# A decoder block on one core: VectorE's small operations set between the maxima of the cross loop, value copy and mask planes moved to ScalarE, value bias to GpSimd

## What is computed

```python
x = x + attn(layernorm(x), Wq, Wk, Wv, Wo)                 # 16 heads of 8, softmax(-arccosh(...))
qh, kh, vh = heads(q @ Wq.T + bq), heads(k @ Wk.T + bk), heads(k @ Wv.T + bv)
scores = einsum('bhqd,bhkd->bhqk', qh, kh) / sqrt(8)
scores = where(mask, scores, -1e9)
x = x + (softmax(scores) @ vh) @ Wo.T + bo                 # the cross block
logits = -dist2(x, keys) + x @ rw.T + rb
topv, topi = top_k(logits, 4); w = softmax(topv)
x = x + sum_j w_j * expert[topi_j](x)                      # gelu, 512 hidden
```

## Time and profile before

| | us |
|---|---|
| median of 3 runs | 865.53 (859.93 to 865.55) |
| the profiled execution | 859.28 |
| its span, first to last instruction | 857.5 |
| the cross loop, first to last of its exponentials (L861) | 376.9 to 646.8 |

### The profile page before, as it was taken

One profiled execution on the slowest core, in us unless ns is written; L12 is line 12 of the kernel. 1 busy time (PEld: TensorE's weight loads), 2 busy tenths in 40 slices (PEclk: granted clock), 3 DMA queues, 4 the chain that ended last, 5 costly groups with the idle time before them and its releaser, 6 DMA issues.

```text
span 857.5 us, 16692 instructions
## 1 busy us (share of the span) xinstructions
PE 713.5 (83%) x5462; PEld 474.6 (55%) x5504; DVE 657.5 (77%) x1662; ACT 578.5 (67%) x747; POOL 477.1 (56%) x578
## 2 busy tenths in 40 slices
PE   3435688797898786999999999999994399999996
PEld 1124455464565553554444444444342399999994
DVE  4669999999899899788788898888745255555554
ACT  2513899999999989245666766657562267777771
POOL 2134887967966797424232634645354366566663
PEclk9855555555555555659999999999997599999999
DMA  9980000000000300051050100000015222222228
GB/s 297 336 274 0 1 1 1 1 0 1 2 1 1 75 0 1 1 157 44 24 169 19 39 25 27 15 17 23 14 33 166 75 60 82 77 79 76 79 79 270
DMA packets 56868, 56.63 MB, mean 66 GB/s; under 512 B 9712, under 2 KB 49520, under 8 KB 56656
## 3 DMA queue, kind: packets, MB, share of 16 engines
q1 hardware_dynamic: 51728, 45.14, 17.9%
q0 software_dynamic: 5056, 10.43, 3.7%
HBM read 25.97 MB, written 29.57 MB: 65 GB/s over the span
## 4 chain that ended last, share of the span: by engine, by line
PE 54%; DVE 24%; issue 12%; POOL 3%; DMA 3%; ACT 2%; SPq 1%; DVEq 0%; POOLq 0%; ACTq 0%
PE ops L1232 7%; PE slot L1337 6%; DVE S_FB L1467 5%; PE slot L1208 5%; DVE S_YZ L1479 4%; PE bps L1350 4%; PE slot L1216 4%; PE ops L1350 4%; PE slot L1045 4%; PE ops L1068 3%; DVE X_junk L1530 3%; DVE S_YZ L1500 3%; PE tps L1194 3%; PE bps L1082 2%; PE bps L1124 1%
## 5 line engine op out<-in xcount | busy, mean ns | idle before, releaser
L606 POOL TENSOR_TENSOR S_YZ<-S_YZ 128x512 f32<-128x512 f32 x128 | 183.0, 1463 | 56.1 <-ACT S_YZ L810 55.9
L861 ACT ACTIVATE B_W<-slot 128x1024 f32<-128x1024 f32 x128 | 131.3, 1026 | 92.5 <-PE slot L1216 92.4
L1530 DVE CUSTOM_DVE_ANT_0 X_junk<-tps,X_MB 128x512 bf16<-128x512 f32 x240 | 156.2, 688 | 31.7 <-PE tps L1194 30.9
L759 POOL DMA_INDIRECT picks<-F_ROUT,F_GOAL x94 | 103.0, 1096 | 70.9 <-DVE F_ROUT L1877 50.2
L1045 PE MATMUL slot<-S_UQT,S_UKT 32*128 32x256 f32 x256 | 84.9, 477 | 52.9 <-DVE S_YZ L1479 52.1
L1045 PEld LDWEIGHTS slot<-S_UQT,S_UKT 32*128 32x128 f32 x256 | 56.7, 298 | 83.2 <-DVE S_YZ L1479 68.7
L1467 DVE TENSOR_SCALAR S_FB<-slot 128x512 f32<-128x512 f32 x128 | 84.6, 684 | 18.5 <-PE slot L1049 18.0
L725 POOL DMA_INDIRECT rows<-B_ROW,B_IDX x64 | 62.7, 980 | 50.3 <-DVE B_ROW L1601 24.2
L1479 DVE SCALAR_TENSOR_TENSOR S_YZ<-slot,S_FB 128x512 f32<-128x512 f32 x128 | 83.5, 683 | 1.9 <-DVE S_FB L1467 0.5
L1049 PE MATMUL slot<-S_GQT,S_GKT 32*128 32x256 f32 x256 | 84.8, 447 | 0.0
L1194 PE MATMUL tps<-X_KFT,X_QFT 24*128 24x512 f32 x240 | 78.7, 519 | 3.4 <-DVE X_MX L1530 1.1
(11 more groups left out here) (300 smaller groups left out, 1595.9 us busy)
## 6 DMA issues: line engine op xcount, KB each, us to landing
rows<-S_blank SPq DMA_DIRECT2D x17, 1040.0 KB, 12.4
F_RIN<-rows SPq DMA_DIRECT2D x47, 130.0 KB, 2.1
B_W<-w1T SPq DMA_DIRECT2D x16, 256.0 KB, 4.4
F_W<-w2T SPq DMA_DIRECT2D x16, 256.0 KB, 4.9
X_CT<-ctxT SPq DMA_DIRECT2D x8, 256.0 KB, 4.7
B_W<-picks SPq DMA_DIRECT2D x8, 256.0 KB, 8.9
B_W<-picks SPq DMA_DIRECT2D x4, 384.0 KB, 5.6
picks<-F_ROUT,F_GOAL POOLq DMA_INDIRECT x94
```

The costliest lines, as they stand in the source:

```text
L606: g.tensor_tensor(Y[:, n % YR], Y[:, n % YR], Zr[:, n % ZR], ALU.add).then_inc(f_rdy, 1)
L861: act.activation(W[:, at:at + 2, 2 * j:2 * j + 2, :].rearrange("p h t n -> p h (t n)"), E_BANKS[k % 2][:, :, :], ACT.Exp, scale=SCALE).the ...
L1530: dve.tensor_tensor_reduce(out=junk[:, i, :], in0=bank, in1=MB[:, c % 2, t, :], scale=1.0, scalar=-3.0e38, op0=ALU.add, op1=ALU.max, accum ...
```

## The change

In the loop VectorE's maxima are called one by one (`maximum_of`), and the small operations, cut into pieces, stand partly between maximum 0 and maximum 1 of a step (`pieces_first`), partly behind maximum 1 (`pieces_second`). The value half of `kv0` and `kv1` (for c >= 2) is copied from `bps` by ScalarE, without its bias, which GpSimd adds in `values`. The mask plane of b + 2 is made by ScalarE in step 10. Batch 7 is called as before.

```diff
-        DVE_KINDS = ("kv0", "kv1", "turn0", "turn1", "lg", "tr", "proj", "pl", "ks", "pq")
+        DVE_KINDS = ("turn0", "turn1", "lg", "tr", "proj", "pl", "ks", "pq")
-        PICK_AT, CHOSEN_AT, WEIGH_AT = at_step(6, 4), at_step(5, 4), at_step(10, 6)
-        STATS_AT, ROOT_AT, REFINE_AT = at_step(12, 8), at_step(13, 9), at_step(14, 10)
+        PICK_AT, ROOT_AT = at_step(7, 4), at_step(13, 9)
...
-                g.tensor_copy(VX[:, c % 2, :, :, 0:8], heads(VST[:, :, :])).then_inc(vx_rdy, 1)
+                g.tensor_tensor(VX[:, c % 2, :, :, 0:8], heads(VST[:, :, :]),
+                                heads(bkv_x[:, D:2 * D].unsqueeze(1).broadcast_to([P, TM, D])), ALU.add).then_inc(vx_rdy, 1)
...
+                if n in ("kv0", "kv1"):
+                    j = int(n[2])
+                    act.wait_ge(k_rdy, 2 * c + j + 1)
+                    if j == 0:
+                        act.wait_ge(vx_rdy, c)
+                    ins = act.copy(VST[:, 2 * j:2 * j + 2, :], src.rearrange("p (t c) -> p t c", c=2 * D)[:, :, D:2 * D])
...
+            def mask_q_next(c):
+
+                act.wait_ge(m_in[c % 2], 16 * (c // 2 + 1))
+                act.wait_ge(mx_rdy, 2 * H * (c - 1))
+                act.activation(MB[:, c % 2], M8[:, c % 2], ACT.Copy, bias=-BIG, scale=BIG).then_inc(mb_rdy, 1)
...
+                    if b + 2 < B and hs == 10:
+                        mask_q_next(b + 2)
...
-            def maximum(c, hs):
+            def maximum_of(c, hs, i):
...
+            def pieces_first(b, hs):
+
+                if hs == 8:
+                    shift_high(b + 1, 0)
+                if hs == 9:
+                    shift_low(b + 1, 0)
+                if b >= 2:
+                    c = b - 2
+                    if hs == 5:
+                        best(c)
+                    if hs == 6:
+                        names(c)
+                    if hs == 7:
+                        equal(c)
+                    if hs == 8:
+                        picks_of(c)
+                    if hs == 10:
+                        place_pick(c)
+                    if hs == 11:
+                        place_index(c)
+                        weigh_inverse(c)
+                if b >= 1:
+                    if hs == 12:
+                        stats_of(b - 1)
+                    if hs == 13:
+                        stats_eps(b - 1)
+                    if hs == 15:
+                        refine_last(b - 1)
+
+            def pieces_second(b, hs):
+
+                if hs == 15:
+                    shift(b + 1, 1)
+                if b >= 2:
+                    c = b - 2
+                    if hs == 4:
+                        logits(c)
+                    if hs == 5:
+                        ranks(c)
+                    if hs == 8:
+                        picked(c)
+                    if hs == 10:
+                        place_sum(c)
+                        weigh_sum(c)
+                    if hs == 11:
+                        weigh_rows(c)
+                if b >= 1:
+                    if hs == 12:
+                        stats_sum(b - 1)
+                    if hs == 14:
+                        refine_first(b - 1)
...
                     if b + 1 < B:
-                        maximum(b + 1, hs)
-                        if hs in (7, 15):
-                            shift(b + 1, hs // 8)
-                    if b + 2 < B and hs == 13:
-                        mask_q(b + 2)
+                        maximum_of(b + 1, hs, 0)
+                        pieces_first(b, hs)
+                        maximum_of(b + 1, hs, 1)
+                        pieces_second(b, hs)
```

More of the change, by code:

```diff
@@ L1508, in keys_values @@
                     wait(dve, kf_rdy, c * 3)
-                    wait(dve, vx_rdy, c)
+                    if c < 2:
+                        wait(dve, vx_rdy, c)
                 src = t_bank(name, c).rearrange("p (t c) -> p t c", c=2 * D)
@@ L1518, in mask_q, with maximum, shift_high @@
                 dve.tensor_scalar(MB[:, c % 2], M8[:, c % 2], 1.0, BIG, ALU.subtract, ALU.mult).then_inc(mb_rdy, 1)
-            def maximum(c, hs):
+            def maximum_of(c, hs, i):
                 h0, t = pair(hs)
                 n = c * HS + hs
-                if hs == 0:
+                if hs == 0 and i == 0:
                     dve.wait_ge(mb_rdy, c + 1)
-                for i in range(2):
-                    wait(dve, mx_rdy, 2 * n + i - 1)
-                    bank, full, count = max_bank(c, hs, i)
-                    dve.wait_ge(full, count)
-                    dve.tensor_tensor_reduce(out=junk[:, i, :], in0=bank, in1=MB[:, c % 2, t, :], scale=1.0,
-                                             scalar=-3.0e38, op0=ALU.add, op1=ALU.max,
-                                             accum_out=MX[:, t, h0 + i:h0 + i + 1]).then_inc(mx_rdy, 1)
-            def shift(c, half):
+                wait(dve, mx_rdy, 2 * n + i - 1)
+                bank, full, count = max_bank(c, hs, i)
+                dve.wait_ge(full, count)
+                dve.tensor_tensor_reduce(out=junk[:, i, :], in0=bank, in1=MB[:, c % 2, t, :], scale=1.0,
+                                         scalar=-3.0e38, op0=ALU.add, op1=ALU.max,
+                                         accum_out=MX[:, t, h0 + i:h0 + i + 1]).then_inc(mx_rdy, 1)
+            def maximum(c, hs):
+                for i in range(2):
+                    maximum_of(c, hs, i)
+            def shift_high(c, half):
                 hs = slice(8 * half, 8 * half + 8)
@@ L1543, in shift, with stats_of @@
                                          op0=ALU.mult, op1=ALU.subtract).then_inc(q2_rdy, 1)
+            def shift(c, half):
+                shift_high(c, half)
+                shift_low(c, half)
             rch = Chain(dve, rt_step)
-            def stats(c):
+            def stats_of(c):
                 dve.wait_ge(*t_emptied("proj", c))
@@ L1562, in refine, with refine_last, logits @@
                 rch.link(dve.tensor_tensor(RT_[:, :], R0[:, :], R0[:, :], ALU.mult))
-                rch.link(dve.tensor_tensor(RT_[:, :], RT_[:, :], VE[:, :], ALU.mult))
+                rch.step(dve.tensor_tensor(RT_[:, :], RT_[:, :], VE[:, :], ALU.mult))
+            def refine_last(c):
+                rch.sync()
                 rch.link(dve.tensor_scalar(RT_[:, :], RT_[:, :], -0.5, 1.5, ALU.mult, ALU.add))
                 dve.tensor_tensor(RSTD[:, :], R0[:, :], RT_[:, :], ALU.mult).then_inc(rs_rdy, 1)
-            def choose(c):
+            def refine(c):
+                refine_first(c)
+                refine_last(c)
+            def logits(c):
                 if c == 0:
@@ L1658, in back_at @@
                     else:
-                        place(b - 1)
+                        place_base(b - 1)
                 elif n == "pl":
@@ L1814, in _ @@
                             back_at(n, c)
-                        elif at == hs and n == "lg":
+                        elif at == hs and n == "lg" and b == B - 1:
                             choose(c)
```

83 lines of the change are left out of this document (63 added, 20 removed).

## The result

The changed kernel takes 868.11 us (median of 20 runs, 865.44 to 874.0), the kernel before 865.01 (20 runs, 859.45 to 868.29). The ratio is 1.0056, 95% interval 1.0038 to 1.0075: some 4.8 us slower, under 1%. The prediction named 868.6, 3.1 us more than before, and "same" as the likeliest class.

The account below looks back on a forecast made before the run. TensorE and VectorE's maxima wait for each other in the cross loop. Loop waits 2.05, GpSimd's rows 0.5 and ScalarE 0.5 sum to 3.05, say 3.1 us, over the 865.53 median: 868.6 us, range 860 to 872.

Parts of the forecast that it names:

- Four constants: Loop hand-off: first maximum 0.65 after its product, second 0.61 later, next product 0.75 after its maximum, TensorE continuing after second product.
- the rule d(next) = 2.01 + p - w - d: Per step: d, TensorE's wait between first score and second maxima products; p, work between maxima; w, TensorE's work before next step.
- Rival (a): In the loop, a piece between the maxima costs nothing and the edit works as meant: 861.5 us; chance 0.12.
- The lengths between: Pieces between the two maxima add their length p, 0.10 to 0.40 us by step; bounds nothing to some +3 more.
- The sum of d: TensorE's waits over batches 1 to 6 of the loop: 19.85 us against 17.8 read, so +2.05 us.
- GpSimd's last rows: After the loop, rows start later because `refine` ends behind maximum 0 of step 15, delaying `n3`: +0.5 us.
- ScalarE: 0.5 forecast: In batches 0 and 1 the mask plane delays ScalarE's copy of `s0`, 0.2 to 0.3 each: +0.5 us, bounds 0 to 2.
- Rival (b): ScalarE's copies miss `bps` in each batch by 0.3 to 1 us: +6 more, 874.5 us; chance 0.08.
- The bias at 0: GpSimd's bias addition, 1.72 us instead of a 0.6 copy, seven times, ends before the wait for the keys: 0.
- (c): Rival with a loss in step 5, its own description omitted from the text; the range to 872 includes it; chance 0.05.
- The total: Whole kernel: 2.05 + 0.5 + 0.5 = 3.05, say 3.1 us slower, median 868.6 us (+0.36%).
- The signature: Loop waits: step 11 0.92 to about 0.25, 13 0.67 to 1.07, 8 and 0 about 0.3; batch 34.6 to 34.7; `n3` 1.1.

Follow-up runs that it names:

- the doubled statistics: Changed kernel with step 12's two statistics made twice, the second time between the maxima (904.97 us) or behind them (909.37 us), one execution each on another chip.
- the moves alone: Kernel before with only ScalarE copying values and making later mask planes, and GpSimd adding the bias; VectorE's small operations unmoved: 865.61 us, ratio 1.0025.

## Why the prediction was right, point by point

- **Four constants and the rule d(next) = 2.01 + p - w - d: held.** In batches 2, 3 and 5 the waits forecast and measured are 0.32 and 0.34 in step 0, 0.12 and 0.12 in 2, 0.59 and 0.59 in 5, 0.29 and 0.28 in 8, 0.25 and 0.28 in 11, 1.07 and 1.06 in 13, 0.12 and 0.11 in 15. Rival (a) is out: a piece between the maxima costs its length, by the doubled statistics too (0.38 for 0.40 us).
- **The lengths between: one wrong.** `shift_low` in step 9 was estimated at 0.11 from its half in step 8; it holds the second maximum 0.22, since it waits for the end of GpSimd's cast and so takes 0.29 instead of 0.19. In batch 6, without the cast, it takes 0.19 and costs the 0.10. Hence 0.31 in step 10 instead of 0.22.
- **The sum of d: forecast 19.85 after, measured 21.00 for batches 1 to 6.** Of the miss of 1.15 `shift_low` is 0.45, some 0.09 in each of batches 1 to 5. One late maximum is 0.34: the second of step 15 in batch 3 starts 0.31 late, with nothing in the profile that it waited for, and step 0 of batch 4 pays. The rest are hundredths of steps that the rule set at 0. The 17.8 that it was set against left out step 15 of batch 6 (0.30) and reads 18.2 by the same weight loads; it also holds a late maximum of 0.35 in step 13 of batch 4 (1.02 instead of 0.67), which the forecast for after let go without a reason. Against 18.2 the forecast term would have been 1.64. Measured: 2.79.
- **GpSimd's last rows: 0.5 forecast, 0.53 measured** (`n3` 5.54 instead of 5.01).
- **ScalarE: 0.5 forecast, about 0.4 measured.** 0.2 in batch 1, as forecast. Batch 0 is 0.35 longer in all, of which its steps 2 and 11 lengthened by 0.1 and 0.2; step 2 differs by up to 0.3 between runs of kernels that are alike there, step 11 is the mask plane's. Batches 2 to 5 show none, as forecast. Rival (b) is out: with the moves alone batches 2, 3 and 5 are the same to 0.04 us.
- **The bias at 0: the step that failed.** The prediction counted the addition as covered by the wait for the keys in each batch. No run shows the loss in step 5 that the chance of 0.05 for (c) and the 872 at the upper end of the range stand for: in the changed kernel the subtraction of step 5 took 0.15 us in each of batches 2 to 6 and started after the addition of `values` had ended, with every piece behind the second maximum it met that addition's last 0.11 to 0.15 us in batches 3 to 6 and took 0.15 to 0.19, and beside the addition the logits' sum kept its 0.19 and the maxima their 0.67 to 0.69. The prediction missed, though the earlier trace rows have a mask plane at 1.32 us beside an addition of GpSimd and at 0.69 alone, that the values of batch 0 are made beside the first normalisation, where VectorE is the one that TensorE waits for: 0.6 us at the transposes, 0.4 to 3.4 at the loop. It also missed the hold by the cast in step 9 (0.29 instead of 0.19). The length it took for the addition, 1.72 us from a like one, measured 1.26 to 1.32, and there are eight of them, not seven.
- **The total.** Loop 3.44, rows 0.53, bias 0.4 to 3.4: 4.4 to 7.4 us, beside 4.8 by the ratio (3.3 to 6.5). The forecast of 3.1 was 1.7 short of the ratio. That it met the median to 0.5 us is luck: the level it started from, 865.53 from three runs, was 0.5 above the median of 20, and the medians differ by only 3.1 where the ratio gives 4.8. The profiled executions differ by 7.7, and 2.7 of it is the stretch in which the clock rose earlier in the one of before.
- **The signature: as written.** Step 11 down to 0.28, 13 up to 1.06, 8 and 0 at 0.3, periods 34.77 where 34.6 to 34.7 was said, `n3` waiting 1.09.

## What to carry to other kernels

In a hand-off over two buffers, the time between the two consumers is on the path in each step whose producer has little other work (0.40 us more there cost 0.38 in step 13), and the time behind the second is free as long as it doesn't push the next pair back (the same 0.40 there cost nothing; `place`, which did push it back, cost step 11 its 0.92). So spread small operations behind the pair, not into it, and take the one that overruns apart. Before an engine is called idle enough to take an operation, look at what its neighbour runs at that moment in each stage, the first pass too: an addition instead of a copy (1.26 us instead of 0.60) made one operation of VectorE 1.20 us long instead of 0.52 where VectorE was the late one. And read the effect of an edit by steps, and outside them between executions that reach the place at the same moment: here the run-to-run difference of the way to the loop (6 us) was larger than any of the effects, and the same addition cost 0.4 us in one group and 3.4 in another.
